# Perceiver block on one core: key and value projections as three fp32r products, values for two groups in one unit, denominators by four transposes

## The reference

```
q = (x @ Wq + bq).reshape(B, N, 16, 32)
k = (y @ Wk + bk).reshape(B, M, 16, 32)      # y: (2, 8192, 384), Wk, Wv: (384, 512)
v = (y @ Wv + bv).reshape(B, M, 16, 32)
scores = jnp.einsum('bnhd,bmhd->bhnm', q, k) / sqrt(32)
attn = jax.nn.softmax(scores, axis=-1)
out = jnp.einsum('bhnm,bmhd->bnhd', attn, v).reshape(B, N, 512)
```

## Time and profile before

| | us |
|---|---|
| median of 3 runs | 3368.82 (3367.44 to 3369.25) |
| the profiled execution | 3372.97 |
| its span in the profile | 3371.2 |
| PE busy | 3229.8 (96%) |
| DVE busy | 2261.7 (67%) |
| ACT busy | 1633.3 (48%) |
| POOL busy | 1839.9 (55%) |

### The profile page before, as it was taken

The page is one execution under the profiler, slowest core; times in us unless marked ns, Lnnn a source line. Parts: engine busy times, 40 slices in busy tenths (PEclk is TensorE's granted clock), DMA queues, the critical chain, the costliest instruction groups (busy, mean ns, idle before and its releaser), DMA issues.

```text
span 3371.2 us, 47005 instructions
## 1 busy us (share of the span) xinstructions
PE 3229.8 (96%) x18328; PEld 2085.4 (62%) x18328; DVE 2261.7 (67%) x3627; ACT 1633.3 (48%) x2869; POOL 1839.9 (55%) x462
## 2 busy tenths in 40 slices
PE   6899999999999999999999999999997869699999
PEld 4676666666676666666676666666643323244477
DVE  5666666666666666666666666666644699995844
ACT  1355555555555555555555555555551447240111
POOL 2477777777777777777777777777780000000000
PEclk9899999999999999999999999999998989799999
DMA  4232222212131233212132222212114012123200
GB/s 132 65 75 48 48 57 51 64 39 57 41 74 48 48 79 76 68 39 57 41 75 48 48 58 51 64 39 58 40 28 157 26 50 101 38 100 139 75 10 19
DMA packets 88717, 204.90 MB, mean 61 GB/s; under 512 B 21744, under 2 KB 23792, under 8 KB 87248
## 3 DMA queue, kind: packets, MB, share of 16 engines
q1 hardware_dynamic: 88496, 201.90, 22.2%
HBM read 90.48 MB, written 6.49 MB: 29 GB/s over the span
## 4 chain that ended last, share of the span: by engine, by line
PE 86%; DVE 10%; issue 1%; SPq 1%; DMA 1%; ACT 1%; POOL 1%; DVEq 0%; ACTq 0%
PE ps L1577 16%; PE ps L1613 14%; PE ps L1603 13%; PE ps L1559 10%; PE ps L1541 9%; PE ps L1562 8%; PE ps L1791 3%; PE ps L1625 3%; PE ps L1755 3%; DVE pm L877 3%; PE ps L1771 2%; PE ps L1590 2%; DVE bx L1111 1%; SPq L547 1%; PE ps L1585 1%
## 5 line engine op out<-in xcount | busy, mean ns | idle before, releaser
L877 DVE TENSOR_REDUCE pm<-ps 128x1 f32<-128x512 f32 x2048 | 1407.2, 691 | 756.7 <-PE ps L1577 753.9
L1318 ACT ACTIVATE pf<-ps 128x512 f32<-128x512 f32 x2048 | 1223.8, 600 | 1040.8 <-PE ps L1603 990.5
L754 POOL TENSOR_TENSOR psum<-psum,pf 128x2048 f32<-128x2048 f32 x256 | 1168.4, 4564 | 235.0 <-ACT pf L1318 224.7
L1577 PE MATMUL ps<-ks,qs 96*128 96x512 f32 x2048 | 996.2, 487 | 27.5 <-DMA ks<-KH 9.2
L1603 PE MATMUL ps<-qs,ks 98*128 98x512 f32 x2048 | 816.4, 400 | 1.8 <-ACT pf L1318 1.6
L754 POOL TENSOR_TENSOR psum<-pf 128x2048 f32<-128x2048 f32 x128 | 584.6, 4567 | 367.5 <-ACT pf L1318 367.4
L1577 PEld LDWEIGHTS ps<-ks,qs 96*128 96x128 f32 x2048 | 392.5, 192 | 269.5 <-issue 224.6
L1559 PEld LDWEIGHTS ps<-cT,Wk 128*128 128x128 f32 x3072 | 489.1, 193 | 92.2 <-issue 12.1
L1562 PEld LDWEIGHTS ps<-Wv,cT 128*128 128x128 f32 x3072 | 470.5, 191 | 67.3 <-issue 0.5
L1559 PE MATMUL ps<-cT,Wk 128*128 128x128 f32 x3072 | 492.2, 276 | 12.9 <-DMA cT<-in_ctxT 12.1
L1613 PE MATMUL ps<-pf,V 128*32 128x512 f32 x4096 | 495.7, 602 | 0.0
(11 more groups left out here) (193 smaller groups left out, 2507.5 us busy)
## 6 DMA issues: line engine op xcount, KB each, us to landing
ks<-KH SPq DMA_DIRECT2D x512, 128.0 KB, 2.4
ks<-KL SPq DMA_DIRECT2D x256, 128.0 KB, 2.4
cT<-in_ctxT SPq DMA_DIRECT2D x32, 768.0 KB, 4.7
BC<-bc_rows SPq DMA_DIRECT2D x32, 512.0 KB, 4.6
ring<-in_ffn_w SPq DMA_DIRECT2D x16, 1024.0 KB, 5.5
wA<-in_W_fcT SPq DMA_DIRECT2D x4, 1024.0 KB, 10.9
wB<-in_W_projT SPq DMA_DIRECT2D x4, 1024.0 KB, 6.6
qs<-q_rows SPq DMA_DIRECT2D x48, 64.0 KB, 2.0
```

Of the source, the lines that this page charges most:

```text
L754: pool.tensor_tensor(acc, before, pf[:, tile % P_SLOTS, :], ALU.add).then_inc(s_sum, 1)
L877: dve.tensor_reduce(pm[:, n // BLK, n % BLK:n % BLK + 1], src, AX.X, ALU.max).then_inc(s_wfree, 1)
L1318: act.activation(pf[:, tile % P_SLOTS, j * NTOK:(j + 1) * NTOK], ps[:, S_BANK + u % S_BANKS, :], ACT.Exp, scale=SCALE).then_inc(s_exp, 1)
L1577: last = pe.matmul(dst, qs[0:3 * HD, h, t * P:(t + 1) * P], ks[0:3 * HD, h, i * 512:(i + 1) * 512], start=True, stop=True)
```

## The change: what it does

Context and weights are split like the keys: a part rounded to fp32r (`cTh`, `Wkh`, `Wvh`, by ACT) and the remainder (`cTl`, `Wkl`, `Wvl`, by DVE, a subtraction of two SBUF operands). A projection is then hi x hi, hi x lo and lo x hi, three fp32r products for each 128 of the 384 input dimensions. `cTl` lies over `cT`, `Wkl` over `Wk` and `Wvl` over `Wv`. A K unit has 9 products with 512 columns; a V unit has 18 products with 256 columns, and makes the values of 256 tokens for two groups at once. The order is K0, V0, K1, V1, and 8 steps of projection begin earlier. To make room, `ks` holds three groups, and a group's key weights are loaded from a scratch in DRAM (`wk_rows`) into `Wkg` by one DMA for each group, issued after `stack_keys`. D is four transposes of the sums instead of four products with a selection of columns.

The diff, cut to its core:

```diff
-SIDE_UNITS = [("K", 0), ("K", 1), ("V", 0), ("V", 1)]
+SIDE_UNITS = [("K", 0), ("V", 0), ("K", 1), ("V", 1)]
 SIDE_AHEAD = 2
 SIDE_SPAN = UPG // len(SIDE_UNITS)
 SIDE_STEPS = SIDE_SPAN - 1
-SIDE_EARLY = 5
-PIECES = 4 * KC
-PIECES_AT = [range(r * PIECES // SIDE_STEPS, (r + 1) * PIECES // SIDE_STEPS) for r in range(SIDE_STEPS)]
+SIDE_EARLY = 13
+TERMS = 3 * KC
+VM = 2
+PIECES = {"K": TERMS, "V": VM * TERMS}
+PIECES_AT = {kind: [range(r * n // SIDE_STEPS, (r + 1) * n // SIDE_STEPS) for r in range(SIDE_STEPS)]
+             for kind, n in PIECES.items()}
+KS = 3
+
+
+SPLIT_AT = {"hi": {34: [(0, 0), (0, 1)], 42: [(0, 2)], 58: [(1, 0), (1, 1)], 60: [(1, 2)]},
+            "lo": {42: [(0, 0)], 50: [(0, 1), (0, 2)], 66: [(1, 0), (1, 1)], 68: [(1, 2)]}}
...
-        ks = sb("ks", [P, NH, CH], F32R, att)
+        with ExitStack() as c:
+            sb("first_keys", [P, (KS - 1) * HG, CH], F32R, c)
+            Wkh = sb("Wkh", [P, KC, D], F32R, c)
+            with ExitStack() as lo:
+                Wk = sb("Wk", [P, KC, D], c=lo)
+            Wkl = sb("Wkl", [P, KC, D], F32R, c)
+        ks = sb("ks", [P, KS * HG, CH], F32R, att)
         KH = sb("KH", [P, CH], F32R, att)
         KL = sb("KL", [P, CH], F32R, att)
-        cT = sb("cT", [P, KC, CH], c=att)
-        V = sb("V", [P, NG, MT * HG, HD], c=att)
+        cTh = sb("cTh", [P, KC, CH], F32R, att)
+        with ExitStack() as c:
+            cT = sb("cT", [P, KC, CH], c=c)
+        cTl = sb("cTl", [P, KC, CH], F32R, att)
+        V = sb("V", [P, 2, MT, 2 * HG * HD], c=att)
...
+            sp.wait_ge(s_wlo, 1)
+            for a, src in enumerate((Wkh, Wkl)):
+                for g in range(NG):
+                    sp.dma_start(wk_rows[g, :, a], src[:, :, g * P:(g + 1) * P].bitcast(F32)).then_inc(s_wsave, 16)
             sp.wait_ge(s_qsave, 32)
+            sp.wait_ge(s_wsave, 2 * NG * 16)
             for g in range(NGT):
-                more = g % NG == 1 and g // NG + 1 < NB * NCH
+                more = g // NG + 1 < NB * NCH
                 if NGB - NG < g <= NGB:
                     next_queries(g - NGB + NG - 1)
                 if NGB - NG + 2 <= g < NGB + 2:
                     save_out(0, g - NGB + NG - 2)
                 if g + SIDE_AHEAD < NGT:
                     stack_keys(g + SIDE_AHEAD)
-                if more:
-                    sp.wait_ge(s_side, side_count(("V", g + 2, 0)))
+                if g == 0:
+                    sp.wait_ge(s_ones, KS)
+                    sp.dma_start(ks[3 * HD:SROWS, (KS - 1) * HG:KS * HG, :].bitcast(F32),
+                                 ks[3 * HD:SROWS, 0:HG, :].bitcast(F32)).then_inc(s_ones2, 16)
+                if g + SIDE_AHEAD + 1 < NGT:
+                    sp.dma_start(Wkg[:].bitcast(F32), wk_rows[(g + SIDE_AHEAD + 1) % NG]).then_inc(s_wkg, 16)
+                if g % NG == 0 and more:
+                    sp.wait_ge(s_side, side_count(("K", g + 3, 0)))
                     load_context(g // NG + 1, 0)
+                if g % NG == 1 and more:
+                    sp.wait_ge(s_side, side_count(("V", g + 2, 1)))
+                    load_context(g // NG + 1, 1)
...
+            def low_context(c, i, f):
+
+                part = slice(i * CH // 2, (i + 1) * CH // 2)
+                dve.wait_ge(s_chi[i], c * KC + f + 1)
+                dve.tensor_tensor(cTl[:, f, part], cT[:, f, part], cTh[:, f, part].bitcast(F32),
+                                  ALU.subtract).then_inc(s_clo[i], 1)
...
-                if side_ends(i - 1):
-                    take_side(side_ends(i - 1))
+                side = side_ends(i - 1)
+                if side and side[0] == "K":
+                    take_side(side)
                 if i + SB_AHEAD < UNITS:
                     probabilities(i + SB_AHEAD)
+                if side and side[0] == "V":
+                    take_side(side)
+                for part in splits_at("hi", i):
+                    high_context(*part)
...
-                    pe.wait_ge(s_ctx[i], (x[1] // NG + 1) * 16)
                     if x in LEAD_SIDE:
-                        pe.wait_ge(s_wkv, 32 if x[0] == "V" else 16)
+                        pe.wait_ge(s_wlo, 2 if x[0] == "V" else 1)
+                    if x[0] == "K" and x[1] > SIDE_AHEAD:
+                        pe.wait_ge(s_wkg, (x[1] - SIDE_AHEAD) * 16)
                 for n in pieces:
-                    m, f = divmod(n, KC)
-                    tokens = slice((4 * i + m) * P, (4 * i + m + 1) * P)
+                    m, n = divmod(n, TERMS)
+                    f, term = divmod(n, 3)
                     if x[0] == "K":
-                        last = pe.matmul(dst[:, m * P:(m + 1) * P], Wk[:, f, g * P:(g + 1) * P],
-                                         cT[:, f, tokens], start=(f == 0), stop=(f == KC - 1))
+                        if term == 0:
+                            context_split(pe, x, f)
+                        w = [a[:, f, g * P:(g + 1) * P] if x[1] <= SIDE_AHEAD else Wkg[:, n, f, :]
+                             for n, a in enumerate((Wkh, Wkl))]
+                        half = slice(i * CH // 2, (i + 1) * CH // 2)
+                        last = pe.matmul(dst, w[term == 2], (cTh, cTl)[term == 1][:, f, half], start=(n == 0),
+                                         stop=(n == TERMS - 1))
                     else:
-                        last = pe.matmul(dst[:, m * P:(m + 1) * P], cT[:, f, tokens],
-                                         Wv[:, f, g * P:(g + 1) * P], start=(f == 0), stop=(f == KC - 1))
-                if pieces[-1] == PIECES - 1:
+                        if m == 0 and n == 0:
+                            context_split(pe, x, KC - 1)
+                        t = VM * (x[1] % 2 * 2 + i) + m
+                        pair = slice(g // 2 * 2 * P, (g // 2 + 1) * 2 * P)
+                        last = pe.matmul(dst[:, m * 2 * P:(m + 1) * 2 * P],
+                                         (cTh, cTl)[term == 2][:, f, t * P:(t + 1) * P],
+                                         (Wvh, Wvl)[term == 1][:, f, pair], start=(n == 0), stop=(n == TERMS - 1))
+                if last_piece(x, pieces):
...
                     pe.wait_ge(s_dt, x[1] + 1)
-                    first_of = ident[:].rearrange("p (j d) -> p j d", d=HD)[:, :, 0]
                     for t in range(NT):
-                        last = pe.matmul(dst[:, t * HG:(t + 1) * HG], dt_[:, t * P:(t + 1) * P], first_of,
-                                         start=True, stop=True)
+                        last = pe.transpose(dst[:, t * P:(t + 1) * P], dt_[:, t * P:(t + 1) * P], ident[:])
```

More of the change, by code:

```diff
@@ L92, in lead_in @@
 def lead_in():
-    side = [(kind, g, i) for kind, g in (("K", 0), ("V", 0), ("V", 1), ("K", 1)) for i in range(2)]
+    side = [(kind, g, i) for kind, g in (("K", 0), ("V", 0), ("V", 1), ("K", 1)) for i in range(2)] + [("K", 2, 0)]
     a = [("A", n) for n in range(A_AHEAD + SB_AHEAD)]
@@ L97, in lead_in @@
     work = a[:first] + [("M", 0)] + a[first:]
-    order = [(x, range(PIECES)) for x in side[:6]]
+    order = [(x, range(PIECES[x[0]])) for x in side[:6]]
     for n, x in enumerate(work):
         order.append((x, None))
-        if n < 2 * PIECES:
-            order.append((side[6 + n // PIECES], range(n % PIECES, n % PIECES + 1)))
+        if n < 2 * TERMS:
+            order.append((side[6 + n // TERMS], range(n % TERMS, n % TERMS + 1)))
+        elif first - 2 <= n < first - 2 + TERMS:
+            order.append((side[8], range(n - first + 2, n - first + 3)))
     return side, work, order
@@ L146, in side_ends @@
     part = side_at(i)
-    return part[0] if part and part[1][-1] == PIECES - 1 else None
+    return part[0] if part and last_piece(*part) else None
 BEFORE_IN_BANK, _seen = {}, {}
@@ L250, in emit @@
         s_hsplit = sem("s_hsplit")
-        s_wkv = sem("s_wkv")
+        s_wk = sem("s_wk")
+        s_wv = sem("s_wv")
+        s_whi = sem("s_whi")
+        s_wlo = sem("s_wlo")
+        s_wsave = sem("s_wsave")
+        s_wkg = sem("s_wkg")
+        s_ones2 = sem("s_ones2")
+        s_chi = [sem(f"s_chi{i}") for i in range(2)]
+        s_clo = [sem(f"s_clo{i}") for i in range(2)]
         s_vch = sem("s_vch")
@@ L512, in keys_stacked, with keys_of, context_split @@
             eng.wait_ge(s_ks[g % NG], (g // NG + 1) * (48 * HG))
+        def keys_of(g, j):
+            return g % KS * HG + j
+        def context_split(eng, x, f):
+            half = x[2] if x[0] == "K" else x[1] % 2
+            eng.wait_ge(s_clo[half], x[1] // NG * KC + f + 1)
         @block.sync
@@ L727, in _ @@
             pool.wait_ge(s_ones, 1)
-            for g in range(NG):
+            for g in range(KS - 1):
                 pool.memset(ks[3 * HD:SROWS, g * HG:(g + 1) * HG, :].bitcast(F32), 1.0).then_inc(s_ones, 1)
@@ L928, in _ @@
                     empty(x)
[L929 removed]
+                elif x[0] == "K" and last_piece(x, pieces):
                     low_keys(x)
@@ L934, in _ @@
                     empty(x)
```

(29 more changed lines are left out.)

65 lines of the change are left out of this document (44 added, 21 removed).

## The result

| | before | after |
|---|---|---|
| median of 7 runs, us | 3369.25 (3367.44 to 3371.33) | 3379.96 (3378.16 to 3383.54) |
| span of the profiled execution, us | 3371.2 | 3378.9 |
| PE busy, us | 3229.8 | 3123.8 |
| DVE busy, us | 2261.7 | 2453.5 |

The ratio is 1.0031, with a 95% interval of 1.0021 to 1.0042: the changed kernel is slower by 0.3%, or 10.7 us, where 71 us (2.1%) faster was forecast. PE is busy for 106 us less, and the span is 8 us longer.

The account below looks back on a forecast made before the run. PE was taken to bound the kernel. The terms 155 + 31 + 2 - 12 - 8 - 97 = 71 us took the profiled 3372.97 to 3302; the median, 4.2 below profiled time, gave 3298 us, range 3192 to 3350.

Parts of the forecast that it names:

- the term of the subtractions: DVE's subtractions in the groups wait for POOL's additions and delay PE: 6.5 us for each of 15 chunks, 97 us lost.
- the term of `Wkg`: The key weights' DMA, 13th behind the keys, lands 0.8 us before PE needs it at step 17: cost 0.
- What bounds the kernel: In the groups PE sets the pace, busy for 37.8 of 37.9 us; a microsecond less per group is worth some 62.
- Values and keys, 155 us: Projection products on PE cost 8.3 us a group instead of 10.8: 2.5 us saved in each of 62 groups.
- The rival to it: V products of 256 columns cost 0.235 us each, as 512 columns do: +270 us, 3568; chance 3%.
- D, 31 us: D on PE becomes as short as T, 0.44 us instead of 0.92: 0.48 saved in each of 64 groups.
- New maximum, 12 us: In step 20 the new maximum holds DVE, and a unit A waits 0.2 us longer: 12 us lost.
- The rival in which it meets POOL: At step 20 a new-maximum instruction waits 4.55 us for POOL's addition; PE loses 3.5 a group, 217 us: 3515; chance 6%.
- The case of 66%: DVE's subtractions in the groups wait for POOL's additions: 3298 us, with its own range of 3262 to 3345; chance 66%.
- its last rival: No change: waits cost twice the count, as delays pass on and PE's clock falls after 3 us waits: about 3369; chance 3%.
- ACT's copies, 8 us: ACT's copies at step 0 stand in front of an exponential: 0.5 us for each of 15 chunks, 8 us lost.
- Lead-in, a gain of 2: Before the groups, extra subtractions and DMAs against idle DVE time, fewer memsets and shorter products: -3 to +3, taken as 2 gained.

Follow-up runs that it names:

- experiment 5: The kernel before with only D changed, to four transposes: 3340.2 us, ratio 0.991.
- experiment 1: The changed kernel without the 90 subtractions of the groups, so keys and values are less exact: 3242.6 us, ratio 0.962 to the kernel before.
- experiment 8: The changed kernel with the groups' subtractions on POOL and the key weights' DMA ahead of the key DMAs: 3226.0 us, ratio 0.957 to the kernel before.
- 2: The changed kernel with the groups' 90 subtractions done by POOL between its own instructions: 3248.8 us, ratio 0.964 to the kernel before.
- experiment 7: The changed kernel with the groups' 90 subtractions reading a PSUM bank as one input, so results are wrong: 3256.7 us, ratio 0.966 to the kernel before.
- experiment 3: The changed kernel with 6 and 12 throwaway products in PE's two long waits of a chunk: 3344.3 us, ratio 0.992 to the kernel before.
- experiment 6: The changed kernel with the key weights' DMA issued ahead of the twelve key DMAs: 3339.0 us, ratio 0.991 to the kernel before.

## Why the prediction was wrong, point by point

The waits were named and came as described. What failed is the term of the subtractions, which priced only the waits of PE and put at nothing what PE's clock does behind them, and the term of `Wkg`, put at 0. By the steps of the prediction:

- *What bounds the kernel.* Right. PE sets the pace, and the time moves by what PE waits.
- *Values and keys, 155 us.* A little high. The group without subtractions is 2.6 us shorter than before, D's part 0.5 of it, so 2.15 are left for projections and the longer wait for the maximum, where 2.5 - 0.2 = 2.3 were forecast. The V product costs 0.12, not 0.115. The rival to it falls: it neither costs 0.235 nor shows a weight load in its spacing.
- *D, 31 us.* Right: 28.7 (experiment 5).
- *New maximum, 12 us.* Right: its wait is 0.34 us for each group where 0.15 to 0.17 stood. The rival in which it meets POOL didn't come: the five instructions end 0.3 us ahead of an addition (1519.85 and 1520.17), the gap that was forecast.
- *`Wkg` in time by 0.8 us, price 0.* Wrong, by some 24 us. PE reaches K0's first product at +12.9 and the DMA goes out at +9.4, as counted (13.0 and 9.5, from unit A of step 8), but it lands 3.3 us after its issue, not 2.7:

```profile
Wkg<-wk_rows SPq DMA_DIRECT2D x61, 384.0 KB, 3.3
```

  So 0.2 us are left of the margin. Where a DMA of the row goes out late (in experiment 1 one of them takes 1.43 us to issue instead of 0.6, at 245.59), or the landing is late, PE waits: by 0.3 to 1.4 us in 19 of the first 60 groups of experiment 1. The first group is worse, with 3.5 us of waiting and 3.4 us at half clock behind it:

```profile
139.31 0.35 SPq L661 DMA_DIRECT2D Wkg<-wk_rows  x1
143.02 0.55 PE L1670 MATMUL ps<-cTh,Wkg 128*128 128x512 f32 x1 [3.51 <-issue]
```

  The DMA was priced against one margin, with a 0 although the bounds reached 1.2; experiment 8 against 2 gives 23 us, 4.5 of them before the first T.
- *The subtractions, 97 us.* **The step that failed most**: 137 to 139 (experiment 1; a chunk takes 152.2 us against 143.1, and the ratios of the two series give 139). The durations on DVE were forecast well (3 to 5 us where POOL adds, 0.65 where not; measured 2.5 to 4.7, 1.6 for the one that waits for the rescaling alone, and 0.68), and so were PE's waits: 2.4 + 3.8 + 0.3 = 6.5 forecast, 0.93 + 1.7 + 2.7 + 0.8 = 6.2 us in the chunk shown and 5.3 in the mean, 79 us in all. Not priced was what PE's standing still does afterwards. In each chunk PE runs for 7.7 us in the mean at 1.2 GHz, behind the wait at K1 and mostly behind that for the weights too. By the split of experiment 1 that costs 3.8 us a chunk, 57 us in all; filling the waits gave back 36. So the two groups with subtractions take 43.8 and 36.5 us, where 37 to 39 were forecast. The prediction had the lower clock in its last rival, as a thing that might double the waits' cost, with 3%. It belonged into the sum: the earlier trace rows told that over the groups PE had never stood still like this, so their clock of 0.99 was no evidence for the changed kernel.
- *ACT's copies, 8 us.* Perhaps double: the first and third periods of a chunk stay 0.75 and 0.35 us above the others in experiment 8, 17 us in all. No run shows that this is ACT: the copy of the values behind a burst is in it, and so are POOL's subtractions, since in experiment 1 the first period is only 0.35 above. I didn't split these.
- *Lead-in, a gain of 2.* About 1: the ninth score product starts at 126.97 us, where it started at 127.99. T of the first group is 2.8 us later than before all the same (174.2), because the wait of 3.5 us for `Wkg` lies in between.

The sum again with these: -145 for projections, -29 for D, +12, +17, +24 for the weights, +137 for subtractions and clock, -1 for the lead-in make +15, where +8 to +11 was measured; the terms come from rounded periods and from different series, and the rest isn't settled. The forecast of 3298 was wrong mainly by 57 us of clock and 24 of weights, while the waits themselves came 18 us cheaper than their 97. The clock alone or the weights alone would have left the kernel faster than before. The case of 66% was right in its waits and wrong in its price. Its own range, up to 3345, allowed a chunk 9 us, close to the 9.1 measured, but without naming the clock as a reason; it is the weights, the smaller gain of the projections and the longer first and third periods that carried the time past 3350.

What stays open: why the half clock lasts 3.4 us in some chunks and 6.8 in others behind the same wait of 2.72 us, and why it follows 10 of the 15 waits for the weights and not the other five.

## What to carry to other kernels

Before DVE work goes into a loop in which POOL is busy, ask of each instruction whether two of its inputs lie in SBUF: if so, price it at the rest of POOL's instruction in flight, find out what is queued behind it on DVE, and try the same work on POOL itself or in a form with a PSUM input. A single SBUF input is no guarantee by itself: the one-input instruction of the earlier trace rows was held for up to 3.63 us beside memsets. Where a change makes a so far unbroken PE wait for microseconds, add to the wait what PE loses afterwards at half its clock. In this case that was half of the time at the lower clock. And a transfer issued at the end of a row of DMAs for the next use on the critical engine goes first, not last.

## What the runs showed of the hardware that I had not expected

- A DVE subtraction of 128 x 512 with both inputs in SBUF takes 0.68 us alone and up to 4.71 beside POOL's 4.57 us additions; with one input in PSUM 0.69 at most, in 90 of 90 (experiment 7). It resumes about half a microsecond before its own end, when POOL's instruction ends. The next POOL instruction then goes ahead of a second subtraction (1.56 us for that one) and waits for the first itself: the rescaling takes 1.40 us there against 1.08.
- POOL does the same subtraction in 1.29 us.
- PE ran at 1.2 GHz for 3.4 or 6.8 us after all 15 waits of 2.72 us and for 3.4 us after 10 of 15 waits of 1.5 to 3.0 us; after those of 0.93 us, no lower clock was seen. Throwaway products in the waits kept it at 2.4 GHz and paid for themselves (experiment 3).
- The time at the lower clock cost half of itself: 3.8 us of 7.7 a chunk (the changed kernel against experiment 1), 3.4 of 6.8 (experiment 6 against 8).
- An fp32r product with 256 columns costs 0.12 us and one with 512 columns 0.235, each with a new weight load of 128 columns: no load shows in the spacing.
